# Table products ahead of the key projection, one batch's recurrence summed on TensorE, tables placed by GpSimd

## What is computed

```python
def _bi_wkv(r, k, v, w, u, time_emb):            # r = x, k = v = side input
    tf = sigmoid(sum(time_emb)); decay = exp(-exp(w)) * (0.5 + 0.5 * tf)
    ek = exp(min(k, 30)); ekv = ek * v
    # nf, df: sums of ekv, ek from the left, times decay each step; nb, db: from the right
    euk = exp(min(u + k, 30))
    num = nf + nb - ekv + euk * v
    den = df + db - ek + euk
    return sigmoid(r) * (num / max(den, 1e-8)) * (0.8 + 0.2 * tf)
# feed-forward, group g: xg = x + soft @ mask_up[g].T; gate = xg @ gate_proj[g].T; up likewise
```

## Time and profile before

| | us |
|---|---|
| three runs | 415.28, 416.05, 416.07 |
| median | 416.05 |
| the profiled execution | 415.59 |
| its span, first to last instruction | 413.8 |

### The profile page before, as it was taken

How to read it: one execution, slowest core, us unless ns; L and a number is a source line. 1 busy time by engine, 2 the same in 40 slices (tenths; PEclk the granted TensorE clock), 3 DMA queues, 4 the chain that set the end, 5 groups by cost and what they waited for, 6 DMA issues and landing times.

```text
span 413.8 us, 6407 instructions
## 1 busy us (share of the span) xinstructions
PE 367.6 (89%) x1952; PEld 295.0 (71%) x1952; DVE 326.0 (79%) x759; ACT 275.6 (67%) x673; POOL 218.7 (53%) x230
## 2 busy tenths in 40 slices
PE   0098869899999799898999997999899999999996
PEld 0097656688878667687787776687687878788884
DVE  8999789988988997599999889476567777665543
ACT  5547789798789497796978879784274434453321
POOL 7260614278524868134693121563269756888832
PEclk9999999999999999999999999999999999999999
DMA  6825300112100304001031000110065433365121
GB/s 207 308 76 197 104 0 3 49 57 99 52 0 2 103 0 154 1 2 51 2 101 40 1 2 0 38 48 32 2 186 160 140 115 97 96 216 166 53 76 51
DMA packets 14209, 31.92 MB, mean 77 GB/s; under 512 B 1872, under 2 KB 4432, under 8 KB 14176
## 3 DMA queue, kind: packets, MB, share of 16 engines
q1 hardware_dynamic: 13888, 31.38, 23.2%
q10 hardware_dynamic: 288, 0.14, 0.1%
HBM read 30.43 MB, written 1.08 MB: 76 GB/s over the span
## 4 chain that ended last, share of the span: by engine, by line
PE 66%; DVE 19%; ACT 11%; issue 3%; DVEq 0%; ACTq 0%
PE ov L1223 7%; PE sc L1201 7%; PE tr L1152 5%; PE proj L1140 4%; PE acc L1126 3%; PE acc L1128 3%; PE acc L1127 3%; PE proj L1144 3%; PE proj L1141 3%; PE acc L1317 2%; PE acc L1318 2%; PE tr L1127 2%; PE acc L1321 2%; PE tr L1126 2%; PE tr L1128 2%
## 5 line engine op out<-in xcount | busy, mean ns | idle before, releaser
L598 POOL TENSOR_TENSOR WL<-stage,WH 128x256 fp32r<-128x256 f32 x142 | 125.6, 913 | 75.6 <-ACT WH L664 75.6
L612 POOL TENSOR_TENSOR PR<-PR,RI 128x512 f32<-128x512 f32 x48 | 53.7, 1134 | 80.7 <-DVE RI L1072 80.7
L1140 PE MATMUL proj<-WH,RH 128*128 128x512 f32 x96 | 42.5, 442 | 32.0 <-DVE RL L923 19.9
L625 ACT ACTIVATE PR<-PR,MX 128x128 f32<-128x128 f32 (+1 forms) x128 | 56.6, 455 | 0.0
L1201 PEld LDWEIGHTS sc<-kT,QT 128*128 128x128 f32 x256 | 41.0, 191 | 15.8 <-issue 12.8
L1223 PE MATMUL ov<-PTS,V 128*128 128x512 f32 x96 | 46.6, 594 | 1.1 <-DVE OL L1084 1.1
L1201 PE MATMUL sc<-kT,QT 128*128 128x128 f32 (+1 forms) x256 | 47.2, 327 | 0.0
L1140 PEld LDWEIGHTS proj<-WH,RH 128*128 128x128 f32 x96 | 18.4, 192 | 38.6 <-issue 36.3
L1062 DVE CUSTOM_DVE_ANT_0 PR<-sc,const,RQ 128x128 f32<-128x128 f32 (+1 forms) x128 | 45.5, 411 | 0.1
L824 ACT CAST OH<-PR 128x512 fp32r<-128x512 f32 x22 | 13.6, 620 | 41.7 <-DVE PR L1108 41.7
L618 POOL TENSOR_TENSOR OL<-PR,OH 128x512 fp32r<-128x512 f32 x22 | 28.9, 1315 | 22.3 <-ACT OH L824 20.8
(11 more groups left out here) (166 smaller groups left out, 948.4 us busy)
## 6 DMA issues: line engine op xcount, KB each, us to landing
stage<-in_ffn SPq DMA_DIRECT2D x22, 384.0 KB, 3.3
stage<-in_wq SPq DMA_DIRECT2D x8, 512.0 KB, 3.3
stage<-in_wo SPq DMA_DIRECT2D x8, 512.0 KB, 3.3
SBC<-group_scalars SPq DMA_DIRECT2D x8, 256.0 KB, 3.6
PR<-in_tables SPq DMA_DIRECT2D x4, 352.0 KB, 7.4
fT<-in_fT SPq DMA_DIRECT2D x4, 256.0 KB, 4.0
xT<-in_xT SPq DMA_DIRECT2D x4, 256.0 KB, 4.5
stage<-in_wk SPq DMA_DIRECT2D x2, 512.0 KB, 4.9
```

What stands on the lines that cost most here:

```text
L598: i = pool.tensor_tensor(lo[:, c:c + 256], src[:, c:c + 256], hi[:, c:c + 256].bitcast(F32), ALU.subtract)
L612: pool.tensor_tensor(pr, pr, RI[:, m % 4, hs[0]:hs[0] + nh].rearrange("p (h o) -> p h o", o=1).broadcast_to([P, nh, 512 // nh]), ALU.mult) ...
L625: return nc.scalar.activation(o, i, ACT.Exp, **k)
L1140: mm(proj[:], rh[ch], wh[ch], start=ch == 0, stop=False, skip_group_check=True)
```

## The change

It does six things.

- START on TensorE: table groups R 0 to 6 run ahead of the first key projection, R 7 between the first and second. All eight have early buffers (6 and 7 in kT, which is written later; the first K3 on ScalarE waits for all groups). Tables are loaded ahead of x of batches 1 to 3; x of batch 0 is issued by ScalarE. The mask is one copy into VX.
- The tables leave acc by two ScalarE copies for each half (into SCRX and SX), and GpSimd places them into EX: one multiplication by table_rest over 352 columns and four additions of 32 partitions, twice. F waits for the copies only.
- The first layer's gate is exp(-x), capped and plus one on GpSimd; it multiplies the denominator, in the operation that also takes its maximum with 1e-8. The full mixing factor takes the place of the half one. The function table with logarithms is loaded at once.
- For batch 1 of the first layer (SUMMED), TensorE adds DF, DB and EUX in the bank sc1 and NF, NB and EU in the bank ov by multiplying with the identity; VectorE reads them there.
- A first-layer projection waits for RH before its first two matmuls and for RL only before the next two.
- New numbers for the places of steps in START, ORDERS, FFN_ORDERS and the background lists.

```diff
-    "PE": [("kv", 0), ("kv", 0), ("kv", 0), ("kv", 0), ("kv", 0), ("D0", 4), ("bg", 0),
-           ("A", 0), ("kv", 0), ("D1", 4), ("kv", 0), ("F", 6), ("E", 5), ("bg", 0),
+    "PE": [("kv", 0), ("kv", 0), ("kv", 0), ("bg", 0), ("D0", 4), ("A", 0), ("kv", 0),
+           ("D1", 4), ("kv", 0), ("E", 5), ("F", 6), ("bg", 0), ("kv", 0), ("C", 1),
...
-    "POOL": [("bg", 0), ("S", 2), ("bg", 0), ("bg", 0), ("rest", 0)],
+    "POOL": [("bg", 0), ("bg", 0), ("bg", 0), ("S", 2), ("bg", 0), ("rest", 0)],
...
+    "PE": [("R", 0), ("R", 1), ("R", 2), ("R", 3), ("R", 4), ("R", 5), ("R", 6),
+           ("K1", 0, 0), ("R", 7), ("split", "K", 0), ("small",), ("split", "Q", 0), ("K1", 0, 1), ("sum", 1, 0),
+           ("sum", 1, 1), ("K3", 0, 0), ("sum", 1, 2), ("K3", 0, 1)],
+    "ACT": [("wkv", 1, 0, 1), ("ex", 0), ("wkv", 1, 0, 6), ("split", "K", 0), ("wkv", 1, 0, 7), ("ex", 1), ("wkv", 1, 1, 1),
+            ("small",), ("split", "Q", 0), ("K1", 0, 0), ("K1", 0, 1), ("K2", 0, 0), ("wkv", 1, 1, 6), ("K3", 0, 0),
+            ("K3", 0, 1), ("wkv", 1, 1, 7)],
+    "DVE": [("wkv", 1, 0, 0), ("wkv", 1, 0, 2), ("wkv", 1, 0, 3), ("wkv", 1, 0, 4), ("wkv", 1, 0, 5), ("wkv", 1, 0, 6), ("wkv", 1, 0, 7),
+            ("wkv", 1, 1, 0), ("split", "K", 0), ("wkv", 1, 0, 8), ("wkv", 1, 1, 2), ("wkv", 1, 1, 3), ("wkv", 1, 1, 4), ("K1", 0, 0),
+            ("K1", 0, 1), ("wkv", 1, 1, 5), ("wkv", 1, 1, 6), ("K2", 0, 0), ("wkv", 1, 1, 7), ("wkv", 1, 1, 8)],
+    "POOL": [("ex", 0), ("split", "K", 0), ("small",), ("ex", 1)],
...
-    for i, st in ((2, ("split", "V", 0)), (0, ("R", 6)), (0, ("R", 7)), (0, ("table", 0)), (3, ("table", 1)),
-                  (2, ("onehot",)), (15, ("zeros",)),
-                  (10, ("split", "K", 1)), (17, ("split", "V", 1))):
+    for i, st in ((2, ("split", "V", 0)), (5, ("table", 0)), (7, ("table", 1)),
+                  (0, ("onehot",)), (13, ("zeros",)),
+                  (10, ("split", "K", 1)), (18, ("split", "V", 1))):
         put(bg, i, st)
+    for b, i in enumerate([0, 0, 2, 5]):
+        put(bg, i, ("ex", b))
...
-    for n, back in enumerate([-2, -2, -2, -1, -3, -2, -2, -3]):
+    for n, back in enumerate([-3, -3, -3, -2, -4, -2, -2, -1]):
         put(bg, max(first_tile(*divmod(n, NKV)) + back, 0), ("split", "Q", n))
...
             side(0)
+            sp.dma_start(mup[:], ins["mup"]).then_inc(s["mup_in"], 16)
+            table(0)
             sp.dma_start(const[:], ins["const"]).then_inc(s["consts_in"], 16)
-            main(0)
-            sp.dma_start(mup[:], ins["mup"]).then_inc(s["mup_in"], 16)
+            table(1)
+            table(2)
+            load(0)
+            table(3)
+            table(4)
+            side(1)
+            table(5)
+            load(1)
+            load(2)
+            table(6)
+            table(7)
             main(1)
             main(2)
             main(3)
...
+                elif st[0] == "ex":
+                    b = st[1]
+                    pool.wait_ge(s["gate_exp"], b + 1)
+                    pool.tensor_scalar(gate1(b), gate1(b), GATE_CAP, 1.0, ALU.min, ALU.add).then_inc(s["gate_ready"], 1)
+                elif st[0] == "table":
+                    h = st[1]
+                    pool.wait_ge(s["table_out"], h + 1)
...
+                    linked(pool.tensor_scalar(SX[:, 0, part], SX[:, 0, part].bitcast(F32), table_rest, None, ALU.mult))
+                    for g in range(4 * h, 4 * h + 4):
+                        rows = slice(32 * (g % 4), 32 * (g % 4) + 32)
...
+                        i = pool.tensor_tensor(EX[rows, h, :, table_col(g):table_col(g) + FI], hi, x, ALU.add)
...
-                    for g in range(4 * h, 4 * h + 4):
-                        rows = slice(32 * (g % 4), 32 * (g % 4) + 32)
-                        i = nc.scalar.copy(EX[rows, h, :, table_col(g):table_col(g) + FI], acc[h][rows, 0:2 * FI].rearrange("p (a n) -> p a n", a=2))
-                    i.then_inc(s["table_hi"], 1)
+                    part = slice(2 * FI * h, 2 * FI * h + 2 * FI)
+                    nc.scalar.copy(SCRX[:, part], acc[h][:, 0:2 * FI])
+                    nc.scalar.copy(SX[:, 0, part], acc[h][:, 0:2 * FI]).then_inc(s["table_out"], 1)
...
             def late_factors():
-                linked(v.tensor_scalar(half_mix[:], tf[:, 3 * B:4 * B], -0.1, -0.4, ALU.mult, ALU.add))
+                linked(v.tensor_scalar(full_mix[:], tf[:, 3 * B:4 * B], -0.2, -0.8, ALU.mult, ALU.add))
+                linked(v.tensor_scalar(half_mix[:], full_mix[:], 0.5, None, ALU.mult))
...
                 elif k == 5:
+                    if summed(L, b):
+                        dve.wait_ge(s["sum_ready"], 2 * SUMMED.index(b) + 1)
+                        dve.wait_ge(s["gate_ready"], b + 1)
+                        done(v.scalar_tensor_tensor(out=DF, in0=sum_bank(b, 0), scalar=1e-8, in1=gate1(b), op0=ALU.max, op1=ALU.mult))
+                        return
...
-                    done(v.tensor_scalar(DF, DF, 1e-8, None, ALU.max))
+                    if L == 1:
+                        dve.wait_ge(s["gate_ready"], b + 1)
+                        done(v.scalar_tensor_tensor(out=DF, in0=DF, scalar=1e-8, in1=gate1(b), op0=ALU.max, op1=ALU.mult))
...
-                wait_r(pe, 2 * p + t // 2, 1)
+                b = 2 * p + t // 2
+                pe.wait_ge(s["wkv_act"], wkv_before(NA, 1, b) + 5)
...
                 for ch in range(CH):
                     mm(proj[:], rh[ch], wh[ch], start=ch == 0, stop=False, skip_group_check=True)
+                wait_r(pe, b, 1)
+                for ch in range(CH):
                     mm(proj[:], rl[ch], wh[ch], start=False, stop=False, skip_group_check=True)
...
+                elif st[0] == "sum":
+                    _, b, k = st
+                    n0 = wkv_before(ND, 1, b)
+                    for x, n, kind in ((DF, 3, 0), (DB, 4, 0), (EUX[:], 5, 0), (NF, 6, 1), (NB, 7, 1), (EU[:], 9, 2)):
+                        if kind == k:
+                            pe.wait_ge(s["wkv_dve"], n0 + n)
+                            i = mm(sum_bank(b, min(k, 1)), ident, x, start=n in (3, 6), stop=n in (5, 9), skip_group_check=True)
```

More of the change, by code:

```diff
@@ L59 @@
     "PE": ["GA", "GB", "Y", "last", "split"],
-    "ACT": ["GT", "split", "last", "GH"],
+    "ACT": ["GT", "last", "split", "GH"],
     "DVE": ["GU", "last", "out"],
-    "POOL": ["split", "GL"],
+    "POOL": ["GL", "split"],
 }
@@ L97 @@
            "route": (0, 1, 3, 4, 6, 7, 8)},
-    "ACT": {"split": None, "small": None, "K1": None, "V": None, "K2": None, "K3": None, "table": None,
+    "ACT": {"ex": None, "split": None, "small": None, "K1": None, "V": None, "K2": None, "K3": None, "table": None,
             "wkv": (1, 6, 7), "gate": (0, 1), "route": (0, 2, 3, 5, 6, 7, 8)},
-    "DVE": {"K1": None, "K2": None, "table": None, "onehot": None, "wkv": (0, 2, 3, 4, 5, 6, 8), "gate": (0, 1),
+    "DVE": {"K1": None, "K2": None, "onehot": None, "wkv": (0, 2, 3, 4, 5, 6, 7, 8), "gate": (0, 1),
@@ L101 @@
             "route": (1, 2, 4, 5, 6, 7)},
-    "POOL": {"split": None, "small": None, "zeros": None},
+    "POOL": {"ex": None, "table": None, "split": None, "small": None, "zeros": None},
 }
@@ L153, in make_plan @@
     ahead = []
-    for f, places in enumerate(([36, 37, 37], [45, 45, 45])):
+    for f, places in enumerate(([36, 39, 39], [45, 45, 45])):
         for kind, i in zip(("GA", "GB"), places):
@@ L218 @@
 PLAN = PLANS["PE"]
-BLOCKS = [s for s in PLAN if s[0] in ("small", "split") or s[0] == "R" and s[1] >= 6]
+BLOCKS = [s for s in PLAN if s[0] in ("small", "split")]
 BLOCK_NO = {s: n for n, s in enumerate(BLOCKS)}
@@ L263, with summed @@
                                       if q[-1] % 2])}
+FIRST_CONST = [st for st in PLAN if st[0] in ("sum", "K3")][0]
+SUMMED = (1,)
+def summed(layer, b):
+    return layer == 1 and b in SUMMED
 NORM_END = [e for q, e in TOK.items() if q[-1] % 2]
-ND = {1: 17, 2: 16}
-NA = {1: 5, 2: 4}
+ND = {call: 12 if summed(*call) else 16 for call in WKV_CALLS}
+NA = {(layer, b): 5 if layer == 1 else 4 for layer, b in WKV_CALLS}
 def wkv_before(count, layer, b):
-    return sum(count[call[0]] for call in WKV_CALLS[:WKV_CALL[(layer, b)]])
+    return sum(count[call] for call in WKV_CALLS[:WKV_CALL[(layer, b)]])
 def last_call(layer, b):
-    return wkv_before(ND, layer, b) + ND[layer]
+    return wkv_before(ND, layer, b) + ND[(layer, b)]
 def item(m):
@@ L900, in wkv @@
                     after(10)
[L901 to L902 removed]
+                    if L == 1:
+                        dve.wait_ge(s["gate_ready"], b + 1)
+                        done(v.scalar_tensor_tensor(out=DF, in0=DF, scalar=1e-8, in1=gate1(b), op0=ALU.max, op1=ALU.mult))
+                    else:
+                        done(v.tensor_scalar(DF, DF, 1e-8, None, ALU.max))
+                elif k == 6:
+                    if summed(L, b):
+                        after(5)
+                        done(v.tensor_tensor(EU[:], EUX[:], f, ALU.mult))
+                        if w == 0:
```

(12 more changed lines are left out.)

171 lines of the change are left out of this document (88 added, 83 removed), and 10 rows, old and new, of the table ORDERS.

## The result

The changed kernel took 411.41 us (median of 4 runs, 410.81 to 412.12), the kernel before beside it 415.69 us (415.28 to 416.07): ratio 0.990, 95% interval 0.988 to 0.992. In later comparisons the kernel before had medians of 415.3 to 415.4 us. The profiled execution of the changed kernel has a span of 409.8 us, 4.0 less than before.

A forecast was written before the change was run, and what follows sets the result against it. Bound: TensorE's work plus idling; VectorE in the opening, shared from 36 to 76 us. Gains 2.0 (opening), 0.5 (later batches), 1.0 (tables), 1.0 (places) sum to 4.5 off 415.59: 411.1, as median 411.3 us; range 405.5 to 417.0.

The forecast's parts named there:

- Opening: Up to the first query projection: shorter recurrences and fewer table matmuls there, less a later x of batch 1, gain 2.0 us.
- The sums' share of the path: Batch 1's recurrence in the opening: TensorE's sums take 1.1 us off VectorE's path ahead of the keys' scaling.
- x of batch 1: Opening: ScalarE's gate waits for this load, queued behind all eight tables; 0.3 us of loss taken out of 0 to 1.5.
- Tables first: Opening: seven table groups before the first key projection take 11.9 us, end at 19 to 20 us and are just free.
- 36 to 76 us: The stage after the opening: placing tables gains 1.1 us on VectorE and 0.5 on ScalarE, less 0.6 for a gate: 1.0.
- Placing the tables: From 36 to 76 us: moving this work off VectorE gains 1.0 us net, with bounds of 0 and 3.4 us.
- New places: Operations reordered on each engine: no row prices this; -3 to +3 us allowed, 1.0 us of gain taken.
- GpSimd late: Rival, tile 5's places: GpSimd's table half, gate and split delay tile 3's probabilities, TensorE stands 6.0 us, 417.5 us; chance 0.14.
- The gate late: Rival, opening not shortened: GpSimd's first-batch gate comes at 16 us, needed by 13.7; 415.1 us; chance 0.09.
- The ring hides it: Rival, one projection bank from 36 to 76 us: only 1.7 us of the opening kept, nothing later; 414.1 us; chance 0.16.
- more than that: Rival: VectorE is the real bound up to 76 us and its whole relief arrives, 8.3 us, 407.5 us; chance 0.18.

The follow-up runs named there:

- e1: The changed kernel with GpSimd clearing EX ahead of its wait for mask_up instead of behind the mask's copy: 410.4 us.
- e3: The changed kernel without TensorE's sums, so VectorE adds up batch 1 itself: 413.65 us.
- e8: e1 with VectorE adding up batch 1 itself, while TensorE does identity products on x of batch 0 that nobody reads: 415.31 us.
- e9: The kernel before with the new orders and background places alone: 413.0 us.
- e5: e1 with the orders and background places of the kernel before, the tables staying at places 5 and 7: 419.7 us.
- e7: e1 with the gate exponential of batch 3, and GpSimd's half of it, at place 6 instead of 5: 414.74 us.
- e6: e1 with the split of query weights 2 at place 6 instead of 5: 412.36 us.
- e4: The changed kernel with the tables placed by ScalarE and VectorE as before, at the new places 5 and 7, none by GpSimd: 415.12 us.
- e12: e1 with VectorE scaling the keys ahead of batch 1's product EU, and TensorE doing both key transposes ahead of the last sum: 411.9 us.
- e13: e5 with the two table halves back at places 0 and 3 instead of 5 and 7: 426.69 us.
- e10: e1 with the split of output weights 0 at place 6 instead of 5: 412.38 us.

## Why the prediction was right, and where it was not

The time (411.3 against 411.41), the sign and the range were right. The sum of terms is right only in total; its terms for the stage up to tile 11 and for the places were far off, in opposite directions.

- *Opening, 2.0 us.* Measured 0.8 at the keys' scaling, 1.3 at the first query projection, 0.6 at tile 0's scores. The terms priced were sound: e1, which differs from the changed kernel only in the clearing, has 2.1, 2.6 and 1.9 us. What the sum left out was that the diff moves GpSimd's clearing of EX beside VectorE's factor operations, 1.3 us in this execution, and that 0.7 us go to ScalarE's queue ahead of the second query projection. The prediction read the added operations of GpSimd and not the moved ones.
- *The sums' share of the path, 1.1 us.* Right as a difference to before: from the reduction of the squares to the keys' scaling VectorE took 4.05 us before (28.81 to 32.86) and 3.04 after (29.00 to 32.04). The 3.1 us of e3 and e8 are another price: the new START puts the whole of batch 1's step 6 ahead of the keys' scaling, so without the sums the numerator's two additions would be on the path too. TensorE's cost (a group of two products 1.72 us, cover by idle time) was right: 5.6 us more work up to tile 0.
- *x of batch 1.* 0.3 us of loss was taken; ScalarE's gate started at 20.32 us, right after RH, without a wait. Tables first: from 8.04 us, seven groups done at 19.42, as worked out, and not on the path.
- *36 to 76 us, 1.0 us of gain.* Wrong in sign: from tile 0 to tile 11 the changed kernel loses 2.0 us net. The gain came (2.0 us from tile 0 to 4), then 3.6 us were lost at tile 5, 2.1 as idling and 1.5 as half clock. The loss is not the new places' alone: on the kernel before they cost 0.9 us there (e9), and the new parts with the old places cost 2.5 us, half clock included (e5). Both have part in ScalarE's queue ahead of V's copy, the parts with a gate of 0.64 us, the places with a second cast of 1.0 us; taken out of it (e7, e6) they shorten the wait by 0.6 and 1.0 us. Nothing in the prediction priced ScalarE's queue at one place; it priced its total. Placing the tables on GpSimd is worth about 3.3 us in e4, not 1.0, but that is against VectorE's pieces at the new places, where they stand in front of the output projection.
- *New places, 1.0 us taken of -3 to +3.* This is the step that failed most: 2.4 us on the kernel before (e9), near the edge of the bounds, and 9.3 us on the new parts (e5), three times as much as they allow. Their gain lies from tile 11 on, 5.2 us, 4.7 of it idling of TensorE, the stage about which the prediction said only that its idle was spread. Which of the moved steps there brings it was not tried.
- *GpSimd late.* It did not come true, and not for the prediction's reason. The rival was to decide once table half, gate and split take more than 9.8 us. They took 1.18 + 3.99, 1.93 and 4.66 us, 11.8 in all, and TensorE still waited only 0.2 us for probabilities from 36 to 113 us. The rule held the queue's start fixed; it began at 65.69 us instead of 68.51, so the probabilities started 5.7 us later and not 9. They were done at 80.02 us, and TensorE asked for them at 81.95: 1.9 us of slack were left.
- *The gate late.* It was ready at 9.40 + 2.26 = 11.66 us and needed at 15.49. The 6 us that the Trainium skill (GPSIMD Engine Reference, section 2.1 Instruction dispatch) has for the first call of a freshly loaded kernel did not appear here: the first tensor_scalar started 0.1 us after its operand was done and took 2.26 us.
- *"The ring hides it" and "more than that".* Both fail by their numbers, and the middle did not give 3.4 us. The first is not wrong in kind: a lead of 2.6 us at tile 4 is gone at tile 5, and in e5, with the old places, one of 2.5 us is gone there too (78.77 against 78.73). But what e1 adds in the opening is not hidden.

So the right total rests partly on luck. Up to tile 11 the sum had a gain of 2.0 + 1.0 = 3.0 us, and the kernel was 1.5 us behind there: 4.5 us too much. After tile 11 it had 0.5 + 1.0 = 1.5 us, and the kernel gained 5.5 (5.2 up to tile 31 and 0.3 behind it): 4.0 us too little.

Put together from the runs: new places alone -2.4 us (e9), new parts alone 4.3 us slower than before even with the early clearing (e5), both together with it -4.9 us (e1). Neither half can be priced without the other.

## What to carry to other kernels

Measure progress at steps that both kernels share, not in fixed windows, and count the work between them: it shows at once whether a gain is kept (the 1.3 us of e1 at tile 0 and at the end), given back (tile 5) or made elsewhere (tiles 11 to 14). An operation that a diff moves needs pricing like one that it adds, on the engine beside it too. With hand-written orders the bound can change from one projection to the next (keys' rows, then batch 1's result, e12), and the numbers in the order lists can be worth more than the work that they place. A wait at one place is not had back for certain by moving what stands before it: four moves of one or two steps eased it, and all cost 2.0 to 4.3 us against the kernel that they were made on.

## What the runs showed of the hardware

- VectorE's 128x4 operation beside GpSimd's memset of 128x768 elements: 1.49 us, against 0.17 without (e1), ending with the memset. In e4 one took 1.92 us beside the mask's copy and the memset, in e3 one took 0.45 us and ended before the memset did, so being held to its end is not the rule. The Trainium skill, GPSIMD Engine Reference, section 1 Specifications, says that the SBUF interfaces are shared and that VectorE instructions in a 2-port mode or with two SBUF inputs contend. This one has a single tensor input; whether it ran in such a mode no row shows.
- GpSimd's one-input operation on 128x512 beside VectorE's scans took 2.26 and 2.83 us, more than its two-input ones of that size (1.12 on average over the kernel, beside scans or not). It had been priced at 1.0.
- GpSimd's copy of the mask as one instruction of 384 columns took 0.51 us; before, eight of 48 columns took 6.15 us beside scans.
- TensorE's granted clock fell to 0.50, of 1.2 and 2.4 GHz the lower, after a wait of 3.42 us (tile 5) and during one of 8.98 us (e3, from 30 us on), and stayed there for about 4 us of work; after 9.4 us (e13) it stayed for 6. The length of a wait does not tell by itself: after 2.19 us it fell in e5, after 2.45 us in e10 (tile 5) and 2.14 before it stayed at 1.00. Nor is idling the whole of it: in e12 and e5 the clock fell at 22 us, while TensorE was at work.
